# Last stage of a gated attention block: expert and attention norm sums interleaved on VectorE, the first norm applied on ScalarE, the gate's bias as a three-row bf16 product

## What is computed

```python
x = x + tanh(g_xattn) * attention(layernorm(x), ctx, ctx)
xn = layernorm(x)
# ffn(xn):
q_in = rope(xn);  q, k, v = q_in @ Wq.T + bq, q_in @ Wk.T + bk, xn @ Wv.T + bv
ctx2 = causal_attention(q, k, v)
x1   = layer_norm(xn + ctx2 @ Wo.T + bo) * ln1_w + ln1_b
gates = softmax(x1 @ gate_w.T + gate_b)                  # 8 experts
moe  = sum over the top 2 of gates[e] * (x1 @ expert_w[e] + expert_b[e])
out  = x + tanh(g_ffn) * (layer_norm(x1 + moe) * ln2_w + ln2_b)
```

## Time and profile before

| what | us |
|---|---|
| three runs | 445.87, 446.86, 446.89 (median 446.86) |
| the profiled execution's own time | 446.81 |
| its span, first to last instruction | 445.0 |
| busy PE | 392.4 (88% of the span) |
| busy DVE | 375.8 (84%) |
| busy ACT | 276.5 (62%) |
| busy POOL | 320.5 (72%) |

### The profile page before, as it was taken

How to read it: one execution, slowest core, us unless ns; L and a number is a source line. 1 busy time by engine, 2 the same in 40 slices (tenths; PEclk the granted TensorE clock), 3 DMA queues, 4 the chain that set the end, 5 groups by cost and what they waited for, 6 DMA issues and landing times.

```text
span 445.0 us, 17674 instructions
## 1 busy us (share of the span) xinstructions
PE 392.4 (88%) x6568; PEld 237.6 (53%) x6568; DVE 375.8 (84%) x1201; ACT 276.5 (62%) x700; POOL 320.5 (72%) x712
## 2 busy tenths in 40 slices
PE   0368988888888899999999999999899999999995
PEld 0144544544544556666666666666655555556552
DVE  6587999999997888887878888777758999999997
ACT  1126777777777766666766766667554757566562
POOL 4456667667779888888788878758704677777784
PEclk9999999999999999999999999999999999999998
DMA  6755696665553343343434343342000000000001
GB/s 165 193 157 156 174 208 169 161 167 140 139 136 96 103 110 98 100 115 106 126 107 110 98 109 105 101 116 66 10 2 1 1 24 24 13 26 13 24 26 48
DMA packets 88037, 42.76 MB, mean 96 GB/s; under 512 B 16000, under 2 KB 87824, under 8 KB 87952
## 3 DMA queue, kind: packets, MB, share of 16 engines
q1 hardware_dynamic: 80864, 39.59, 33.7%
q10 hardware_dynamic: 7088, 2.04, 2.0%
HBM read 5.69 MB, written 2.10 MB: 17 GB/s over the span
## 4 chain that ended last, share of the span: by engine, by line
PE 47%; ACT 4%; DVE 4%; issue 3%; POOL 1%; POOLq 0%; ACTq 0%; DVEq 0%
PE s_bank L920 7%; PE u_bank L499 7%; PE st_bank L920 6%; PE s_bank L421 4%; PE u_bank L942 4%; PE s_bank L434 4%; DVE r L697 2%; PE u_bank L940 2%; PE u_bank L906 2%; PE t_bank L413 2%; ACT z_x_t L1017 2%; PE t_bank L407 2%; PE u_bank L514 1%; ACT part L577 1%; PE t_bank L408 1%
## 5 line engine op out<-in xcount | busy, mean ns | idle before, releaser
L716 DVE TENSOR_REDUCE nm<-s_bank 128x4 f32<-128x512 f32 x256 | 171.6, 683 | 36.8 <-PE s_bank L434 34.3
L599 ACT ACTIVATE pt<-st_bank 128x512 f32<-128x512 f32 x250 | 147.5, 602 | 74.3 <-PE st_bank L434 52.5
L434 PE MATMUL s_bank<-qk 64*64 64x128 bf16 (+1 forms) x1584 | 103.7, 221 | 11.5 <-DVE nm L716 4.3
L499 PE MATMUL u_bank<-pt,vaug 128*32 128x128 f32 x2048 | 108.6, 286 | 1.9 <-issue 0.2
L434 PE MATMUL st_bank<-qk 64*64 64x128 bf16 (+1 forms) x1540 | 98.5, 219 | 0.2 <-issue 0.2
L434 PEld LDWEIGHTS s_bank<-qk 64*64 64x64 bf16 (+1 forms) x1584 | 73.9, 104 | 35.4 <-issue 19.4
L434 PEld LDWEIGHTS st_bank<-qk 64*64 64x64 bf16 (+1 forms) x1540 | 69.3, 103 | 0.4 <-issue 0.4
L499 PEld LDWEIGHTS u_bank<-pt,vaug 128*32 128x32 f32 x2048 | 41.3, 108 | 28.0 <-issue 5.9
L421 PE MATMUL s_bank<-mqk,idb 64*64 64x256 bf16 x256 | 38.3, 292 | 0.5 <-ACT pt L599 0.4
L327 POOL TENSOR_TENSOR part<-r,part 128x512 bf16<-128x512 f32 x32 | 37.0, 1158 | 1.4
L421 PE MATMUL st_bank<-mkq,idb 64*64 64x256 bf16 x244 | 35.7, 293 | 0.0
(11 more groups left out here) (133 smaller groups left out, 810.8 us busy)
## 6 DMA issues: line engine op xcount, KB each, us to landing
qk<-part SPq DMA_DIRECT2D x221, 128.0 KB, 2.7
x_all<-x SPq DMA_DIRECT2D x16, 128.0 KB, 2.7
qk<-qrow SPq DMA_DIRECT2D x32, 64.0 KB, 2.1
c_all<-ctx_in SPq DMA_DIRECT2D x14, 128.0 KB, 2.8
out<-z_o SPq DMA_DIRECT2D x14, 128.0 KB, 1.8
qk<-mts ACTq DMA_DIRECT2D x34, 32.0 KB, 2.9
qk<-mts SPq DMA_DIRECT2D x30, 32.0 KB, 2.1
ewt<-exp_t SPq DMA_DIRECT2D x1, 512.0 KB
```

Source lines behind the costliest of these rows:

```text
L434: ins = pe.matmul(to[outs, :], fixed[:, outs], moving, start=not masked, stop=True, skip_group_check=masked)
L499: ins = pe.matmul(u_bank[b][32 * j:32 * j + 32, r * P:(r + 1) * P], v, pt[m % 4][:, j, :], start=half == 0, stop=half == 1, skip_group_che ...
L599: act.activation(pt[m % 4][:, :, :].rearrange("k j q -> k (j q)"), transposed_bank(m)[:, :], ACT.Exp).then_inc(ex, 1)
L716: dve.tensor_reduce(nm[q % 2][:, first:first + HEADS], s_bank[n % 2][:, :].rearrange("q (j k) -> q j k", j=HEADS), AX_X, ALU.max, negate=T ...
```

## The change

In words: (1) `normalise1` of groups 2 to 15 moves from VectorE to ScalarE, behind the gate exponentials; it needs an offset, so `factor1` on POOL issues two more instructions for these groups. (2) The gate's bias is split into three bf16 parts, put into three rows (`gbs`) by eleven POOL instructions ahead of slot 232, and added by a product of three rows of ones with `gbs` ahead of the logits. The add of L1136 is gone; the maximum and the exponentials read PSUM. TensorE therefore waits for the exponentials, no longer for the add, before it overwrites these columns. (3) The two pairwise sums of gated experts get a second level on VectorE (`gated_sum`), so TensorE adds one operand with the identity, no longer two. (4) The add, statistics and moments of `attention_sum` and `all_experts` alternate.

```diff
@@ POOL, attention stage
+            def split_gate_bias():
+                rest = gbb
+                for k in range(PARTS):
+                    pool.tensor_scalar(gbp[k][:, :], rest[:, :], 1.0, 0.0, ALU.mult, ALU.add).then_inc(c_gb, 1)
+                    if k < PARTS - 1:
+                        pool.wait_ge(c_gb, 2 * k + 1)
+                        pool.tensor_tensor(gbr[k][:, :], rest[:, :], gbp[k][:, :], ALU.subtract).then_inc(c_gb, 1)
+                        pool.wait_ge(c_gb, 2 * k + 2)
+                        rest = gbr[k]
+                pool.wait_ge(c_gb, 2 * PARTS - 1)
+                for k in range(PARTS):
+                    pool.tensor_scalar(gbr[k][:, :], gbp[k][:, :], idf[:, k:k + 1], 0.0, ALU.mult, ALU.add).then_inc(c_gb, 1)
+                pool.wait_ge(c_gb, 3 * PARTS - 1)
+                pool.tensor_tensor(gbr[0][:, :], gbr[0][:, :], gbr[1][:, :], ALU.add).then_inc(c_gb, 1)
+                pool.wait_ge(c_gb, 3 * PARTS)
+                for b in range(G):
+                    pool.tensor_tensor(gbs[:, b * NE:(b + 1) * NE], gbr[0][:, :], gbr[2][:, :], ALU.add).then_inc(c_gb, 1)
+
             for n in range(FIRST_SLOT, DRAIN):
                 ...
+                if s == UNITS - 3 and t == 0:
+                    split_gate_bias()
                 q = seq_at(n, 4)
                 if q is not None:
                     max_split(q)
@@ TensorE, last stage
             def transpose_n(g, gc):
                 ...
                 if gc == 1:
                     pe.wait_ge(z_x1c, 1)
-                    pe.wait_ge(z_gate, 1)
+                    pe.wait_ge(z_exp, 1)
             def logits(g, gc):
                 pe.wait_ge(z_x1c, g + 1)
                 ...
                 if gc >= 1:
-                    pe.wait_ge(z_gate, (g - 1) * GATE + 1)
+                    pe.wait_ge(z_exp, g)
                     pe.wait_ge(z_gtc, g)
+                pe.wait_ge(c_gb, 3 * PARTS + G)
+                pe.matmul(logit_columns(g), krow[0:PARTS, 0:P], gbs[0:PARTS, :], start=True, stop=False)
                 for b in range(G):
                     ins = pe.matmul(logit_columns(g)[:, b * NE:(b + 1) * NE], zx1t[i][:, b * P:(b + 1) * P], gwt[:, :],
-                                    start=True, stop=True)
+                                    start=False, stop=b == G - 1)
             def gated_sum(g, gc):
                 pe.wait_ge(z_gtc, g + 1)
-                pe.wait_ge(z_yp, g + 1)
                 ...
                 pe.matmul(dst, zgt[i][:, :], ebs[:, :], start=True, stop=False)
-                for e in range(HALF // 2):
-                    ins = pe.matmul(dst.rearrange("q (b d) -> q b d", b=G), idf[:, :], zyp[:, :, e, :],
-                                    start=False, stop=e == HALF // 2 - 1)
-                ins.then_inc(z_yb, 1)
+                pe.wait_ge(z_yq, g + 1)
+                pe.matmul(dst.rearrange("q (b d) -> q b d", b=G), idf[:, :], zyq[:, :, :],
+                          start=False, stop=True).then_inc(z_yb, 1)
@@ ScalarE
+            def normalise1(g, gc):
+                i = gc % 2
+                act.wait_ge(z_rs, rstd_steps(g + 1))
+                act.wait_ge(z_nt, g - 1)
+                act.wait_ge(z_x1, (g - 2) * 2 + 1)
+                for b in range(G):
+                    act.activation(zn[i][:, b, :], zh[i][:, b, :], ACT.Identity, bias=znb[i][:, b:b + 1],
+                                   scale=zrs[i][:, b:b + 1]).then_inc(z_n, 1)
             def gates_exp(g, gc):
-                act.wait_ge(z_gate, g * GATE + 2)
+                act.wait_ge(z_gate, g * GATE + 1)
                 for b in range(G):
-                    ins = act.activation(zp[:, b, :], zl[:, b, :], ACT.Exp, bias=zm[:, b:b + 1])
+                    ins = act.activation(zp[:, b, :], logit_columns(g)[:, b * NE:(b + 1) * NE], ACT.Exp, bias=zm[:, b:b + 1])
             def body(s, c):
                 if in_z(c, 2):
                     gates_exp(s - 2, c - 2)
+                if in_z(c, 1):
+                    normalise1(s - 1, c - 1)
                 if in_z(c, 0):
                     copy_att(s, c)
@@ VectorE
             def shift_logits(g, gc):
                 dve.wait_ge(z_lg, g + 1)
-                dve.tensor_tensor(zl[:, :, :], logit_columns(g).rearrange("q (b e) -> q b e", b=G),
-                                  gbb[:, :].unsqueeze(1).broadcast_to(per_seq), ALU.add).then_inc(z_gate, 1)
-                dve.wait_ge(z_gate, k + 1)
-                dve.tensor_reduce(zm[:, :], zl[:, :, :], AX_X, ALU.max, negate=True).then_inc(z_gate, 1)
+                dve.tensor_reduce(zm[:, :], logit_columns(g).rearrange("q (b e) -> q b e", b=G), AX_X, ALU.max,
+                                  negate=True).then_inc(z_gate, 1)
             def gating(g, gc, second_level=None):
                 ...
                 for b in range(G):
                     dve.match_replace(zq[:, b, :], z8[:, b, :], zp[:, b, :], 0.0).then_inc(z_gate, 1)
+                if second_level is not None:
+                    gated_sum(*second_level)
                 ...
+            def gated_sum(g, gc):
+                dve.wait_ge(z_yp, g + 1)
+                if gc >= 1:
+                    dve.wait_ge(z_yb, g)
+                dve.tensor_tensor(zyq[:, :, :], zyp[:, :, 0, :], zyp[:, :, 1, :], ALU.add).then_inc(z_yq, 1)
             def body(s, c):
                 ...
                 if in_z(c, 2):
-                    gating(s - 2, c - 2)
-                if in_z(c, 1):
-                    normalise1(s - 1, c - 1)
+                    gating(s - 2, c - 2, (s - 3, c - 3) if s - 3 < LAST else None)
                 if in_z(c, 2):
                     experts(s - 2, c - 2)
                 if in_z(c, 0):
-                    attention_sum(s, c)
+                    attention_add(s, c)
+                    experts_add(s - 3, c - 3)
+                    attention_stats(s, c)
+                    experts_stats(s - 3, c - 3)
+                    attention_moments(s, c)
+                    experts_moments(s - 3, c - 3)
+                elif in_z(c, 3):
+                    all_experts(s - 3, c - 3)
@@ POOL, last stage: factor1
-                rstd_of(pool, zmv[i][:, :, 1], zve[i][:, :], zrs[i][:, :], z_rs, g * 2)
+                rstd_of(pool, zmv[i][:, :, 1], zve[i][:, :], zrs[i][:, :], z_rs, rstd_steps(g))
+                for b in range(G if g >= 2 else 0):
+                    pool.wait_ge(z_rs, rstd_steps(g) + 2)
+                    pool.tensor_scalar(znb[i][:, b:b + 1], zmv[i][:, b, 0:1], zrs[i][:, b:b + 1], -1.0,
+                                       ALU.mult, ALU.mult).then_inc(z_rs, 1)
```

More of the change, by code:

```diff
@@ L73, in gated_block_kernel @@
         bvb = sb("bvb", [P, P]); bob = sb("bob", [P, P])
-        gwt = sb("gwt", [P, NE]); gbb = sb("gbb", [P, NE])
+        gwt = sb("gwt", [P, NE]); gbb = sb("gbb", [P, NE]); gbs = sb("gbs", [P, G * NE], BF16)
+        gbp = [sb(f"gbp{i}", [P, NE], BF16) for i in range(PARTS)]; gbr = [sb(f"gbr{i}", [P, NE]) for i in range(PARTS)]
         ewt = sb("ewt", [P, NE * P]); ebs = sb("ebs", [G * NE, W])
@@ L119, in gated_block_kernel @@
         c_tanh = sem("tanh_ready"); c_half = sem("exponent_set"); c_two = sem("expert_bias_zeroed")
-        c_mst = sem("max_stacks_set"); c_low = [sem(f"lower_set{i}") for i in range(RING)]; c_val = [sem(f"value_columns_set{i}") for i in range(RING)]
+        c_mst = sem("max_stacks_set"); c_gb = sem("gate_bias_split"); c_low = [sem(f"lower_set{i}") for i in range(RING)]; c_val = [sem(f"value_columns_set{i}") for i in range(RING)]
         c_late = sem("later_constants_loaded"); c_l2 = sem("last_norm_gated"); c_w = sem("weights_permuted")
@@ L803, in gated_block_kernel @@
         zh = two("z_h", [P, G, P])
-        zst = two("z_stats", [P, G, 6]); zmv = two("z_mv", [P, G, 2]); zve = two("z_ve", [P, G]); zrs = two("z_rstd", [P, G])
+        zst = two("z_stats", [P, G, 6]); zmv = two("z_mv", [P, G, 2]); zve = two("z_ve", [P, G]); zrs = two("z_rstd", [P, G]); znb = two("z_offset", [P, G])
         zn = two("z_n", [P, G, P])
@@ L814, in gated_block_kernel @@
         zrs2 = two("z_rstd2_", [P, G]); znb2 = two("z_offset2_", [P, G]); zy = two("z_y2", [P, G, P]); zyw = sb("z_yw", [P, G, P]); zyc = two("z_yc", [P, G, P])
-        zsum = two("z_x1_moe", [P, G, P]); zyg = sb("z_gated", [P, G, HALF, P]); zyp = sb("z_gated_pairs", [P, G, HALF // 2, P]); zo = [sb(f"z_o{i}", [P, G, P]) for i in range(4)]
+        zsum = two("z_x1_moe", [P, G, P]); zyg = sb("z_gated", [P, G, HALF, P]); zyp = sb("z_gated_pairs", [P, G, HALF // 2, P]); zyq = sb("z_gated_sum", [P, G, P]); zo = [sb(f"z_o{i}", [P, G, P]) for i in range(4)]
         z_ot = sem("z_att_transposed"); z_otc = sem("z_att_t_copied")
@@ L821, in gated_block_kernel @@
         z_gate = sem("z_gate_steps"); z_exp = sem("z_gate_exp"); z_gt = sem("z_gates_transposed")
```

(25 more changed lines are left out.)

26 lines of the change are left out of this document (11 added, 15 removed).

## The result

The changed kernel takes 448.56 us (median of 7 runs, 447.43 to 449.40) beside 446.74 for the kernel before (7 runs, 445.71 to 447.05): ratio 1.0041, 95% interval 1.0028 to 1.0054. It is slower by 0.4%, where 445.2, a gain, was forecast. The profiled execution took 448.17, with a span of 446.4 (before: 446.81 and 445.0). Names of lines have moved: experts L946, gated sum L965 and L967, bias product L930, logits L932, transposes of the rows L918.

A forecast was written before the change was run, and what follows sets the result against it. TensorE was taken to bound the rounds (7.03 us each), VectorE close behind. Rounds -4.9, end -0.1 and startup +3.45 gave -1.6 against 446.8: 445.2, own range 443.9 to 446.6, widest 442.6 to 448.7.

The forecast's parts named there:

- What the startup pays: One-time cost on TensorE ahead of the rounds: POOL's split, wait for exponentials, two groups' bias products; +3.45 us (2.2 to 4.1).
- (a): Eleven POOL instructions ahead of slot 232's split make TensorE's transpose late: +1.7 us, bounds 1.2 and 2.2.
- (b): Drain step DRAIN+2: group 1's transposes wait for group 0's exponentials on ScalarE: +1.6 us (0.8 to 1.8).
- TensorE's part of a round: Per round, two gated-sum instructions fewer save 0.48, the bias product adds 0.07: 7.03 becomes 6.62 us.
- Do the others fit: VectorE, POOL, ScalarE within 6.62: the `normalise2` path makes the rows' copy 0.05 late, so rounds of 6.65 us.
- Body 16 and the end: Last body: two TensorE instructions fewer, same wait for `normalise2`, new add in VectorE's last gating; -0.1 us (-0.5 to +0.4).
- Rival 3: In the rounds, POOL's first power holds VectorE's pairs: rounds of 6.92, 448.7 us, slower; chance 0.17.
- Rival 2: Path over POOL and `normalise2` later, POOL losing time to VectorE's add: rounds of 6.80, 447.2 us, no change; chance 0.25.
- Rival 1: The startup's delays are hidden, as POOL and VectorE have idle time there: 441.8 us; chance 0.10.
- rival 4: TensorE gains 0.53 a round, pays 0.03 for the bias, nothing is late: rounds of 6.53, 443.6 us; chance 0.08.
- Slower: Outcome that the whole kernel gets measurably slower: chance 0.21, from rival 3 (0.17) and rival 2's upper end (0.04).
- signs that the forecast named as proof against it: One of two startup waits missing or made good, pairs starting after the first power's end, or rounds exceeding 6.77.

The follow-up runs named there:

- before_split: The kernel before plus only the eleven POOL instructions of the bias split ahead of slot 232, result unused: 449.01 us, ratio 1.0058.
- before_wait: The kernel before with only group 1's transposes waiting for group 0's gate exponentials, not for the bias add: 449.22 us, ratio 1.0053.
- np_no_interleave: `no_product` with all attention sums first and the experts' sums after them, no longer alternating: 443.08 us, ratio 0.9920.
- np_norm_back: `no_product` with the first norm of all groups back on VectorE and no new offsets on POOL: 441.76 us, ratio 0.9891.
- ab_both: The changed kernel with the bias split moved to slot 235 and group 0's logits copied to SBUF by VectorE: 443.62 us, ratio 0.9938.
- no_product: The changed kernel without bias split and bias product; VectorE adds the bias again and TensorE waits for that add: 441.55 us, ratio 0.9893.
- second_level_only: The kernel before plus only the second-level sum on VectorE; no split, bias product, moved norm or interleave: 447.20 us, ratio 1.0017.

## Why the prediction was wrong

The forecast's sum was -1.6 and the profiled execution's +1.4, of which 0.45 is scatter ahead of the changed part. The measured 448.56 lies inside the widest range stated (442.6 to 448.7), but as a loss where a gain was forecast. By the forecast's own steps:

- **What the startup pays** is the step that failed: +3.45 with an upper bound of 4.1, and 5.0 came (5.45 less the 0.45 of scatter). The two waits were sized right, (a) 1.7 against 1.76 and (b) 1.6 against 1.67. What was missing is a term: a TensorE that stands still for 1.6 to 1.7 may run on at half the clock. That cost 1.26 in the profiled execution, and `before_split` and `before_wait` show it with one stall each. The bounds went by the sizes of POOL's steps and by whether the waits might be hidden, not by what would follow them. (The lower bound of 1.2 in (a) does not follow from its terms either: eleven steps of 0.2 less 0.39 are 1.8. Nothing hung on it.)
- **TensorE's part of a round**: mechanism right, sizes off. The two products gave 0.43 to 0.44, not 0.48, and the bias product took 0.11, not 0.07: 6.71, not 6.62. The first lay just outside its bounds (0.45 to 0.53), the second inside (0.02 to 0.15); over thirteen rounds they are 1.2.
- **Do the others fit**: the 0.03 a round for a late `normalise2` did not come; in the thirteen rounds ScalarE never waited for that offset, though the offset came no earlier than ScalarE was free (390.36 and 390.34). The interleave puts the experts' moments at about the time of the attention's, and POOL's second power took 0.78. The rest of the path was as forecast: first power 0.70, offsets 0.50, norm 0.88. Taken together the rounds gave -4.16, not -4.9. I credited VectorE's relief to the norm's move; the runs showed that the interleave alone would do.
- **Body 16 and the end**: +0.12, not -0.1, within its range. The add in the last gating was named; that POOL's elementwise instructions would hold it and the subtraction was not.
- **The chances.** Rival 3 is refuted: the pairs start 0.17 after a power and take 0.69. Its time, 448.7, is nearly the measured one, by luck: it put into the rounds (6.92) what lay in the startup. Rival 2 did not come in this kernel: rounds of 6.71, not 6.80, and the late path that it names binds only in other kernels (`np_no_interleave`, two rounds of `np_norm_back`). Rival 1 is refuted by `ab_both`, rival 4 by the sizes of 0.43 and 0.11. "Slower" hung on rival 3 (0.17) and the upper end of rival 2 (0.04); the mechanism that decided, the clock behind a stall, had no chance of its own. None of the signs that the forecast named as proof against it came either: both waits were there, the pairs started ahead of the first power's end, and the rounds stayed below 6.77.

## What to carry to other kernels

An edit that opened a stall of 1.6 to 1.7 on a busy TensorE cost here the stall and, in part of the executions, about three microseconds at half the clock behind it (1.0 to 1.3 more); put one-time preparation where its engine idles, and let independent work stand ahead of a new wait. Small terms on the bounding engine are to be taken from the start-to-start distance and multiplied by the rounds before they are called small: 0.11 a round was 1.4 here, for an add that was free on VectorE. When several edits come together, take one away at a time: of four, the gated sum and the interleave carried the whole gain, and the bias product turned it into a loss.

## What the runs showed of the hardware

- Behind a stall of 1.6 to 1.7 of a busy TensorE the granted clock is half for about three us in some executions and full in others of the same kernel; by their mean clock the slower halves are 1.0 (`before_split`) and 1.3 (`before_wait`) above the faster ones. The same fall stands behind a gap of 0.75 in `no_product`.
- Independent instructions on VectorE overlap and dependent ones don't: in `np_norm_back` the experts' sum starts at 385.93, where the attention's ends at 386.01, and in `second_level_only` the statistics of the attention's sum start at 389.00, where that sum ends at 388.97. Ten instructions took 1.72 alternating between two chains and 2.24 with one chain after the other (start of the first to start of the next one behind them). The Trainium skill says in "VectorE: DVE Perf Modes", section "The DRAIN you can't avoid", that the next operation doesn't start until the pipe is empty, and in the same paragraph that one that is not held starts earlier. For the independent instructions the traces agree with the second statement.
- In these traces POOL and VectorE (with both inputs in SBUF) hold each other according to when each starts and to the kind of POOL's instruction. A power that starts 0.02 behind VectorE's pairs takes 1.23, and one that starts 0.01 ahead of them 1.25; pairs that start 0.17 behind a power take their usual 0.69; a VectorE add or subtraction that starts inside an elementwise POOL instruction of 128x256 is held at least to near its end (0.73 for 0.41, ending 0.28 behind POOL's, and 0.69 for 0.17, ending 0.03 behind).
